# End of the first routed stage: VectorE sums a token's two expert results, TensorE turns the sum with one transpose per half

## The reference

```
probs = softmax(x @ w_router); vals, idx = top_k(probs, 2); vals = vals / sum(vals)
for e in range(16):
    gate, up = split(x @ w_gate_up[e])
    out = out + combine[:, e] * ((silu(gate) * up) @ w_down[e])
h = h + out
```

## Time and profile before

| | us |
|---|---|
| median of 3 runs | 989.31 |
| lowest, highest | 989.10, 990.08 |
| the profiled execution, its time | 982.86 |
| its span in the trace, first to last instruction | 981.0 |
| TensorE busy (matmuls) | 860.6, 88% |
| VectorE busy | 442.3, 45% |
| ScalarE busy | 388.6, 40% |
| mean granted clock of TensorE | 0.95 of full speed |
| end of this stage's work on VectorE | 499.76 |

### The profile page before, as it was taken

One profiled execution on the slowest core, in us unless ns is written; L12 is line 12 of the kernel. 1 busy time (PEld: TensorE's weight loads), 2 busy tenths in 40 slices (PEclk: granted clock), 3 DMA queues, 4 the chain that ended last, 5 costly groups with the idle time before them and its releaser, 6 DMA issues. The chain is left out here.

```text
span 981.0 us, 17283 instructions
## 1 busy us (share of the span) xinstructions
PE 860.6 (88%) x6192; PEld 613.7 (63%) x6193; DVE 442.3 (45%) x947; ACT 388.6 (40%) x862; POOL 169.2 (17%) x190
## 2 busy tenths in 40 slices
PE   7888889999982499999898889999998999885997
PEld 5556657677662167777676557764685666662676
DVE  6477757787614022222167675550113666611011
ACT  2466643454421122233154755544133555421332
POOL 0600004554302412222100012310000000003021
PEclk9999999999995699999999898999999999986999
DMA  9700000000029841111230047000000211103111
GB/s 309 194 2 1 2 1 2 1 1 1 2 56 253 255 129 48 48 49 49 90 93 1 1 103 188 2 1 27 1 1 1 63 49 51 49 5 100 33 49 33
DMA packets 39389, 57.46 MB, mean 59 GB/s; under 512 B 4053, under 2 KB 32901, under 8 KB 39321
## 3 DMA queue, kind: packets, MB, share of 16 engines
q1 hardware_dynamic: 27800, 41.63, 15.5%
q10 hardware_dynamic: 8016, 7.20, 2.7%
q0 software_dynamic: 3504, 7.69, 2.3%
HBM read 43.28 MB, written 13.23 MB: 58 GB/s over the span
## 5 line engine op out<-in xcount | busy, mean ns | idle before, releaser
L78 PE MATMUL banks<-con 128*128 128x512 f32 (+1 forms) x204 | 94.9, 579 | 16.0 <-POOLq L1958 14.4
L1798 PE MATMUL banks<-moe_wu,moe_xf 96*128 x256 | 91.4, 502 | 1.3 <-SPq L1745 0.8
L623 PE MATMUL banks<-x,a_wqkv 96*96 96x272 f32 x288 | 74.5, 396 | 1.9 <-PEq L84 1.9
L1798 PEld LDWEIGHTS banks<-moe_wu,moe_xf 96*128 96x128 f32 x256 | 47.2, 194 | 31.0 <-issue 4.2
L78 PEld LDWEIGHTS banks<-con 128*128 128x128 f32 x204 | 38.7, 203 | 42.2 <-issue 38.3
L142 ACT ACTIVATE ln_sq<-x 96x544 f32<-96x544 f32 x32 | 21.0, 657 | 97.0 <-DVE x L134 96.9
L922 ACT ACTIVATE a_vt<-banks 102x384 f32<-102x384 f32 x96 | 42.1, 488 | 41.5 <-PE banks L699 40.9
L623 PEld LDWEIGHTS banks<-x,a_wqkv 96*96 96x96 f32 x288 | 45.5, 165 | 19.4 <-issue 4.4
L699 PE MATMUL banks<-con,a_vx 96*102 96x96 f32 x384 | 44.2, 258 | 7.9 <-ACT a_vt L922 5.7
L1965 POOL DMA_INDIRECT y_rows<-moe_ys,moe_back x32 | 30.8, 962 | 115.7 <-DVE moe_part L2059 110.8
L2069 DVE TENSOR_TENSOR moe_hid<-banks,moe_gs 128x384 f32<-128x384 f32 x32 | 17.9, 558 | 63.2 <-PE banks L1798 55.5
(11 more groups left out here) (387 smaller groups left out, 1758.8 us busy)
## 6 DMA issues: line engine op xcount, KB each, us to landing
moe_wu<-in_moe_up SPq DMA_DIRECT2D x16, 576.0 KB, 10.2
f_w<-in_f_e SPq DMA_DIRECT2D x10, 576.0 KB, 14.7
moe_wd<-in_moe_down SPq DMA_DIRECT2D x16, 288.0 KB, 11.5
moe_x_slots<-slots_zeros SPq DMA_DIRECT2D x1, 3104.0 KB, 23.8
moe_xs<-moe_x_slots ACTq DMA_DIRECT2D x32, 97.0 KB
patch_px<-in_patches SPq DMA_DIRECT2D x4, 768.0 KB, 9.4
f_wu<-in_f_up SPq DMA_DIRECT2D x4, 582.0 KB
f_x_slots<-slots_zeros SPq DMA_DIRECT2D x1, 2310.0 KB, 31.6
```

The lines of the kernel that those rows point to most:

```text
L78: self.nc.tensor.matmul(self.ps[bank][:, 0:width], self.ident, self.con[:, 0:width], start=True, stop=True)
L623: last = nc.tensor.matmul(ps[2 + m][0:HD, 0:CW], wqkv[:, a, j * D + m * HD:j * D + (m + 1) * HD], chunk(x, c)[:, a], start=a == 0, stop=a ...
L1798: last = nc.tensor.matmul(ps[2 + 2 * p + u][:, 0:BW], xf[0:KU[a], p, a], wu[0:KU[a], bass.ds(e, 1), a, u * BW:(u + 1) * BW].rearrange("p e ...
```

## The change

VectorE gets five additions, one per pair of tiles, each of which waits for `y_back` itself and writes the sum of both experts' rows over the first expert's rows. TensorE waits for the sums (`summed`) instead of the loads, and turns a half tile with one transpose instead of two accumulating matmuls. Transposes of a tile: two, where there were four matmuls. Two padding products of 256 columns are put in, behind tiles 1 and 3. On VectorE the sums stand ahead of additions: sums 0 and 1, additions 0 and 1, sum 2, additions 2 and 3, sum 3, addition 4, centring 0, sum 4, additions 5 and 6, and then as before.

```diff
@@ stage_routed_ffn, semaphores
+        summed = sem("summed")
@@ TensorE
             def turn_out(t):
-                pe.wait_ge(y_back[t // 2], 32)
+                pe.wait_ge(summed, t // 2 + 1)
                 if t >= 4:
                     pe.wait_ge(added, t - 3)
                 n = rows(t)
                 for a in range(2):
-                    for k in range(K):
-                        last = nc.tensor.matmul(ps[2 + t % 4][0:HD, a * RT:a * RT + n], yb[k][0:n, t, a * HD:(a + 1) * HD], env.ident[0:n, 0:n],
-                                                start=k == 0, stop=k == K - 1)
+                    last = nc.tensor.transpose(ps[2 + t % 4][0:HD, a * RT:a * RT + n], yb[0][0:n, t, a * HD:(a + 1) * HD], env.ident[0:n, 0:n])
                 last.then_inc(out_turned, 1)
...
                 env.idle_products(6, 3)
                 for t in range(5):
                     turn_out(t)
+                    if t % 2:
+                        env.idle_products(1, 7, width=256)
                 ln.mean(pe, 0)
@@ VectorE
+            def sum_rows(b):
+                dve.wait_ge(y_back[b], 32)
+                n, w = rows(2 * b), min(2, NR - 2 * b)
+                both = [yb[k][0:n, 2 * b:2 * b + w] for k in range(2)]
+                V.tensor_tensor(both[0], both[0], both[1], ALU.add).then_inc(summed, 1)
...
             if norm_out:
-                for t in range(5):
-                    add(t)
+                sum_rows(0)
+                sum_rows(1)
+                add(0)
+                add(1)
+                sum_rows(2)
+                add(2)
+                add(3)
+                sum_rows(3)
+                add(4)
                 ln.centre(dve, 0)
+                sum_rows(4)
                 add(5)
                 add(6)
                 ln.centre(dve, 1)
```

## The result

| | before | changed |
|---|---|---|
| median of 12 runs, us | 986.78 (982.58 to 993.84) | 984.52 (977.04 to 994.50) |
| the profiled execution, its time and span | 982.86, 981.0 | 985.80, 984.0 |
| mean granted clock in it | 0.950 | 0.945 |
| ratio, with its 95% interval | | 0.9947 (0.9921 to 0.9973) |

What follows compares the result with a forecast made beforehand. The prediction took turning matmuls delaying VectorE's additions, and TensorE's low clock, as the bound; 982.86 - 0.55 = 982.3 us in the profiled execution, and the median's 6.45 above it gave 988.8 us, range 986.9 to 991.0.

Steps and rivals of the forecast that it cites:

- What bounds the stage: Stage end behind the last expert tile: VectorE's additions wait for turning matmuls on TensorE, whose low clock matters as much.
- the landing of pair 2: Load wait on VectorE, hidden before and now exposed: forecast at 488.9, setting sum 2 at 488.93 to 489.50.
- the 12.1 us of waiting: VectorE's addition (L2099), from the last expert tile to the next stage: total wait ascribed to the turning matmuls (L1832).
- My rebuild: Stage end re-timed in the new order on both engines: first mean product at 489.95 instead of 490.58, 0.63 us left.
- I take the return at 494.6: TensorE's full clock returning inside the second mean product: stage end 499.2, 0.55 us less; chance 0.32.
- 905 to 911: Earlier stretch used as comparison: six fully busy us passed at clock 0.50, with transposes and gaps ahead of them.
- rival 1: TensorE's clock returns with the first products or is spared: about 2.05 us less, 987.3 us; chance 0.20.
- The padding: Two 256-column products on TensorE, 0.85 us each at the low clock, beside landings and sums: cost the path nothing.
- the 3.1 us at the low clock: TensorE from 484.60 to 487.7 at clock 0.50 after its idle wait: 15 passes ran where 28 would.
- Rival 2: Clock low through both norms until the last padding: TensorE closes the stage, 2.4 us later, 991.7 us; chance 0.13.
- 877.7 to 883.7: Stretch cited for a clock staying low: TensorE fully busy, almost all transposes, clock at 0.50 throughout.
- Rival 4: A later stage gains or loses a slow stretch, about half of 3.1 us, sign unknown; chance 0.10, half each side.

Runs made afterwards that it cites:

- e9: Changed kernel with each 256-column padding product replaced by four 128x128 transposes; sum 2 to end 8.58 us, stage length 19.11 us.
- e10: Same kernel as e9, run again; sum 2 to end 8.46 us, stage length 19.29 us.
- a_again: Changed kernel run a second time with no edit; stage length 19.93 us, ratio 0.9943.
- e6: Changed kernel with eight instead of six padding products ahead of the first tile; stage length 19.14 us, ratio 0.9977.
- a_third: Changed kernel run a third time with no edit; stage length 18.59 us, ratio 0.9967.
- e1: Changed kernel without the two 256-column padding products between the transposes; stage length 22.09 us, ratio 0.9997.
- e5: Kernel before with eight instead of six padding products ahead of the first tile; stage length 21.57 us, ratio 0.9998.
- e8: e4 with eight padding products instead of six and centring 0 ahead of sum 2; stage length 19.02 us, ratio 0.9970.
- b_again: Kernel before, run again with no edit; stage length 22.56 us, whole run 994.01 us.
- e2: Changed kernel with each half tile turned by a matmul against the identity instead of a transpose; stage length 20.48 us, ratio 0.9970.
- e7: Changed kernel with every sum computed twice, the extra one into an unread buffer; stage length 20.22 us, ratio 0.9978.
- e4: Changed kernel with first mean product and centring 0 ahead of tile 4, additions 2 and 3 ahead of sum 2; stage length 19.39 us, ratio 0.9965.

## Why the prediction was wrong

**What bounds the stage, right.** The turning was on VectorE's path, and the landing of pair 2 took its place. Of the 12.1 us of waiting that I quoted for it, though, some 7.0 were the wait for the first pair. My rebuild had the first mean product at 489.95, 12.96 us after the first padding product; it came at 12.50, 12.41 and 10.98 us in the three profiles.

**The step that failed: "I take the return at 494.6".** I compared the new burst with 905 to 911 and said that half of it is transposes and that the wait for pair 2 breaks it. But in e9 and e10 the clock came back behind transposes alone, and the return came before the wait could break the burst: the low stretch lasted to 493.9 in the changed kernel's time, 11.7 us after the first padding product, where my forecast had it 17.6 us after (494.6 - 476.99). The term was worth 2.05 - 0.55 = 1.5 us, and it measured nothing: sum 2 to end is 8.46 in the profiles with a low stretch (changed, a_again) and 8.45 and 8.55 in those without one (e6, a_third). With it goes the forecast: rival 1, to which I gave 0.20, is what happened. Its own sum of 2.05 less is 0.7 short of the first profile.

**What made up the 0.7.** One term of the sum was mis-sized, by 0.3, and one came out 0.4 shorter in this execution. I put VectorE's instructions one behind another at their full durations: 0.42 for an addition and 0.57 for a sum. Back to back they start 0.32 (two additions in 0.74) and 0.47 apart (494.94 to 495.41), since the next begins before the duration of the last is over. From the start of sum 2 to the end I had 8.77 us at the full clock (488.93 to 497.7), measured 8.46, 8.46 and 8.55. And I had pair 2 taken 11.94 us after the first padding product (488.93 - 476.99), from its issue and landing time; it was taken after 11.55 in the first profile and after 11.47 and 10.04 in the two others of the changed kernel. The 0.4 is thus one landing of a time that varies.

**The padding, wrong in its worth.** "They cost the path nothing" was right. That they hold 2 us of the gain (e1: 8.46 against 10.42) stood nowhere in the sum; it put a price on what they cost and none on what they do for the clock. The course of e1, with the clock back 17.8 us after the first padding product, is the one that I had forecast with the padding in (17.6).

**Where the old time went.** I named the 3.1 us at the low clock as part of what bounds the kernel, but gave no price to its moving off the path. e5 shows what it was: 1.5 to 1.7 us of the old stage. The new order has it beside the wait for pair 2, where it costs nothing. So of the 2.8 to 3.2 us gained about a half is this, and about a half (1.6 between e5 and e6) is shorter turning; with one profile of each and landings that vary, the shares are rough.

**The rivals.** Rival 2 did not come true. The Trainium skill, "TensorE: Matmul & The Clock Gate", section "Part 4: PE-mode transpose", would have transposes not count as the engine being busy in the way matmuls do; in e10 an unbroken burst of transposes alone was followed by the full clock, and the measurement decides. What remains open is the row from which I argued for it: from 877.7 to 883.7 TensorE ran fully busy at 0.50 with almost nothing but transposes, of 96 columns and 96 rows. No run changed that stretch. Rival 4 was real in size but not in place: two low stretches of 10 us came ahead of the change, in one profile and not in the other.

**The range.** It reached 2.4 us down because rival 1 was summed at 2.05 and the scatter of low stretches elsewhere was taken at 0.4 to 0.7. One profile alone differed by 5 us from that cause. The base moved as well: the forecast of 988.8 hung on a median of 989.31 from three runs, and the median of twelve, these three among them, is 986.78. Of the 4.3 us between the forecast and 984.52, 2.5 are this, and not an effect of the change.

## What to carry to other kernels

Where an engine waits for loads and its clock falls, ask which of the following work is on the path: a slow burst that ended before the next landing cost nothing here, and the padding that closed its holes held most of the gain (2 of 2.8 us). Measure a change of a few microseconds inside the profile, from one fixed instruction to another and from the last landing on, and in more than one profile: here the whole span pointed the wrong way. When an instruction is moved ahead in one engine's queue, look at what that instruction itself waits for; e8 lost 1.2 us to centring 0.

## What the runs showed that I had not expected

The same instructions with the same data took 5 us more or less ahead of the change, by low stretches at 60 and 101 us that came in some executions and not in others: none in the kernel before's first profile, both in the changed one's, one of them (60.80 to 67.40) in a_third's. The change is not their cause: b_again, the kernel before, was at 0.50 at the same places (up to 65.0, and from 101.4 to 108.0), and e6 and e10, which have the change, were not. The windows of a_third:

```profile
60.80:67.40 6.60, 6.60 (x49) 5.26 (x41) 1.95 (x4) 3.57 (x9) 0.00 (x0) 0.50 0.00 0
101.40:104.70 3.30, 3.30 (x27) 2.06 (x28) 3.30 (x3) 0.63 (x2) 0.00 (x0) 1.00 0.00 0
```

The fall of the clock ahead of the first tile is as loose: of the eleven profiles of kernels with six padding products there, it came in eight and stayed away in a_third, e2 and e7. The landing of pair 2, where sum 2 waited for it, was taken between 10.04 and 11.67 us after the first padding product. The stage lengths of e4 and e8 are 0.6 and 1.0 us below the first profile of the changed kernel, but its own three profiles reach from 18.59 to 20.01, and neither e4 nor e8 was faster than it over whole runs (ratios 0.9965 and 0.9970, intervals 0.7 and 0.6% wide). So no gain of the early mean product is shown.
